# A six-stage decoder on one core: the column add of the switched attention moved by one batch, and other forms of the decay and the coupled attention

## The chip, the core and the metric

One core of a Trainium2 chip runs the whole program: TensorE multiplies, VectorE, ScalarE and GpSimd work elementwise, SyncE issues transfers, and semaphores order them. The metric is the device time of one execution in microseconds.

## The reference

Six layers follow each other, each with a residual and a layer normalisation. The text below is cut to the three attentions that the change touches.

```python
x = _layernorm(x + decay_attention(x))          # 16 batches, 112 tokens, 256 columns
x = _layernorm(x + cross_attention(x, ctx))
x = _layernorm(x + experts(x))
x = _layernorm(x + coupled_attention(x))
x = _layernorm(x + cross_attention(x, ctx))
x = _layernorm(x + switch_attention(x))

# decay attention, one head of 256 columns
qkv = x @ Wqkv + bqkv
attn = softmax(einsum('bqd,bkd->bqk', q, k) / sqrt(256) * mask)   # mask = gamma ** (i - j), 0 above the diagonal
out = einsum('bqk,bkd->bqd', attn, v) @ Wproj + bproj

# coupled attention, 16 heads of 16 columns
attn_scores = einsum('bhid,bhjd->bhij', Q, K) / scale
QJ = einsum('bhid,hde->bhie', tanh(Q), J_attn)
attn_scores = attn_scores + lambda_attn * einsum('bhie,bhje->bhij', QJ, tanh(K))
out = einsum('bhij,bhjd->bhid', softmax(attn_scores), V)          # then @ Wo.T + bo

# switched attention, 8 heads of 128 columns, 8 experts a head
gate_v, gate_o = two best of 8 sigmoid(x @ sel.T), normalised      # per token and head
v = einsum('bshep,bshe->bhsp', einsum('bsd,hedp->bshep', x, v_w), gate_v)
ctx = einsum('bhqk,bkhp->bqhp', softmax(q k^T * SCALE), v)
out = einsum('bshep,hepd->bsd', ctx[..., None, :] * gate_o[..., None], o_w)
```

## The kernel before

Each layer is a stage with its own tiles and semaphores, and a barrier stands between two stages. In a stage every engine has its own program, written out in the order in which it runs. `T` is 112 tokens, `B` 16 batches, `CB` 4 batches make a chunk of `CT` = 448 columns, and there are `NC` = 4 chunks.

**Decay attention** (`stage_decay_attention`, four chunks). TensorE's `step(c)` computes the scores of chunk `c` (L271), turns the normalised rows of chunk `c - 1` (`turn_out`, L263), projects queries, keys and values of chunk `c + 1` (`project`, L245 and L253), turns the probabilities (L280), multiplies them with the values (L287) and then with the output weights (L293). VectorE's `step(c)` makes the probabilities (L350 to L358), adds the output (L367), takes statistics and writes the rows `xn` (L380), all for chunk `c`. Chunks 1 and 2 run in a hardware loop. The decay mask is made by GpSimd at the start (L229).

**Coupled attention** (`stage_coupled_attention`, 16 batches in four groups of four heads). The scores of a group are two products into one bank: queries with masked keys (`km`, L1101), and the coupled queries `qj` with the masked tanh of the keys (`knm`, L1103). A mask keeps 16 of the 128 rows for each head, so that one product covers four heads. VectorE makes `km` (L1292, eight instructions a batch), ScalarE adds the biases to queries and keys (L1203, L1206) and makes `qn` (L1210) and `knm` (L1215, eight). `front` is the work on batch `b + 1`, `tail` that on batch `b - 1`; both are slipped in between the groups of batch `b`. GpSimd takes the inverse root of the variance (L1044) and copies rows (L1046).

**Switched attention** (`stage_switch`, 8 heads x 16 batches = 128 slots `g`). In a slot TensorE computes the values of one batch in two halves (`values(p, b, 0)` and `values(p, b, 1)`, six matmuls of 512 columns each), and between them twelve output matmuls of one unit (`outputs(u)`, a unit is two of the eight experts of one chunk). Large products are split in three (`split_product`, L104 to L106) from a high and a low part. Four units fill the two banks `OUTPUTS`. The units trail the values by two chunks: `gated_at(g)` is the unit whose gate product (`by_gates`, L2557) is made in slot `g`, `multiplied_at(g)` the unit that TensorE multiplies there. ScalarE rounds the gated product to `gh` (`high`, L2467), GpSimd takes the remainder `gl` (`low`, L2286). VectorE's `add_columns(n)` (L2565 for the first head, L2568 for the others) adds the banks to the columns `yt` once a chunk's four units are done, in the slot that `added_at` gives; TensorE's `outputs` waits for it (`y_read`) before the first unit of the next chunk. VectorE also scales and sums the values of a batch (L2523, then the halves in L2528 and L2532), and works through `choose`, the choice of the next head's gates, two steps a slot. `turned_at(g)` says when a chunk's columns are turned back to rows and normalised.

## Time and profile before

| what | us |
|---|---|
| median of 3 runs | 2683.79 |
| lowest, highest | 2677.88, 2686.36 |
| profiled execution | 2682.9 |
| its span | 2681.2 |
| decay attention in it, from 15.7 to 134 | 118.3 |
| coupled attention, from 970 to 1280 | 310 |
| switched attention, from 1690 to 2681 | 991 |

All rows below are of the profiled execution. Times are microseconds from the start of its span, and means are nanoseconds. A row of the timeline merges like instructions that follow each other; in brackets stands how long the engine was idle before it and what released it. A float32 matmul appears as two records. The granted clock of TensorE is 1.00 at 2.4 GHz and 0.50 at 1.2 GHz.

### The profile page before, as it was taken

The page shows a single profiled execution, that of the slowest core. Times are in us where ns is not written, and L with a number is a line of the kernel's source. Part 1 is how long each engine was busy: PE and PEld are TensorE (multiplying, and loading weights), DVE is VectorE, ACT ScalarE, POOL GpSimd, SP SyncE. Part 2 cuts the span into 40 slices and gives each one's busy share as a digit, 9 for nine tenths or more (in the row PEclk, how much of TensorE's full clock was granted, in tenths as well). Part 3 has the DMA queues.
Part 4 walks back from the last instruction along what each step waited for, and adds up shares of the span by engine and source line. Part 5 has one row for each costly group of instructions (what it writes and reads, how often), then busy time and mean ns, then how long its engine had stood idle before and what let it go on. Part 6 is the DMA issues. An engine that isn't in the chain of part 4 may idle for free. (4 is left out here: it accounts for less than half of the span.)

```text
span 2681.2 us, 48451 instructions
## 1 busy us (share of the span) xinstructions
PE 2334.2 (87%) x15579; PEld 1885.1 (70%) x15579; DVE 1741.8 (65%) x4378; ACT 1342.6 (50%) x3314; POOL 462.9 (17%) x382
## 2 busy tenths in 40 slices
PE   7689999869999868887799998889989998999995
PEld 5467777658999755554677776677777777777774
DVE  2356766657888556666467676767676676767555
ACT  2156666645666435554566666434343433434341
POOL 3010000011111320000100000022222323232223
PEclk9799999979999979999899999899999999999998
DMA  3056655224666210000565563232231322222222
GB/s 105 0 136 127 123 120 120 58 81 138 218 211 207 83 53 1 0 0 0 136 126 123 121 122 82 73 90 71 90 94 67 94 82 83 78 85 76 70 63 69
DMA packets 201755, 246.49 MB, mean 92 GB/s; under 512 B 58481, under 2 KB 176706, under 8 KB 201602
## 3 DMA queue, kind: packets, MB, share of 16 engines
q1 hardware_dynamic: 198050, 235.37, 33.6%
q0 software_dynamic: 3552, 9.18, 1.2%
q8 instruction: 84, 1.38, 0.2%
q14 instruction: 69, 0.57, 0.1%
HBM read 202.95 MB, written 41.55 MB: 91 GB/s over the span
## 5 line engine op out<-in xcount | busy, mean ns | idle before, releaser
L793 ACT ACTIVATE cross_pr<-cross_sc,cross_mn 112x375 f32<-112x375 f32 x512 | 310.5, 607 | 231.2 <-DVE cross_mn L883 230.2
L2286 POOL TENSOR_TENSOR switch_gl<-switch_gb,switch_gh 128x896 fp32r<-128x896 f32 x128 | 275.3, 2151 | 682.6 <-ACT switch_gh L2467 682.6
L883 DVE CUSTOM_DVE_ANT_0 cross_sc<-cross_ps,cross_masked 112x375 f32<-112x375 f32 x512 | 272.8, 543 | 177.0 <-PE cross_ps L681 156.1
L2523 DVE SCALAR_TENSOR_TENSOR switch_vt<-switch_ps,switch_chosen,switch_vt 112x128 f32<-112x128 f32 x512 | 144.3, 344 | 281.9 <-PE switch_ps L106 276.5
L104 PE MATMUL switch_ps<-switch_gh,switch_ow 128*128 128x448 f32 x512 | 202.9, 396 | 99.4 <-DVE switch_yt L2568 67.6
L689 PE MATMUL cross_ps<-all_ident,cross_pr 112*125 112x112 f32 x1536 | 255.2, 275 | 23.5 <-DVE cross_pt L890 21.7
L689 PEld LDWEIGHTS cross_ps<-all_ident,cross_pr 112*125 112x125 f32 x1536 | 232.7, 189 | 45.2 <-DVE cross_pt L890 27.7
L681 PE MATMUL cross_ps<-cross_k,cross_q 96*112 96x376 f32 x512 | 221.9, 434 | 14.1 <-DMA cross_k<-cross_k_dram 11.0
L104 PE MATMUL switch_ps<-switch_vw,switchgates_xh 128*112 128x512 f32 x512 | 211.6, 413 | 5.1 <-ACT switch_vt L2446 5.1
L106 PE MATMUL switch_ps<-switch_vw,switchgates_xl 128*112 128x512 f32 x512 | 203.5, 398 | 0.0
L105 PE MATMUL switch_ps<-switch_vw,switchgates_xh 128*112 128x512 f32 x512 | 203.5, 397 | 0.0
L106 PE MATMUL switch_ps<-switch_gh,switch_ow 128*128 128x448 f32 x512 | 200.9, 392 | 0.0
L105 PE MATMUL switch_ps<-switch_gl,switch_ow 128*128 128x448 f32 x512 | 200.6, 392 | 0.0
L104 PEld LDWEIGHTS switch_ps<-switch_gh,switch_ow 128*128 128x128 f32 x512 | 103.6, 202 | 126.8 <-issue 95.1
L2446 ACT ACTIVATE switch_vt<-switch_ps,switch_chosen 112x128 f32<-112x128 f32 x512 | 146.0, 367 | 93.3 <-PE switch_ps L106 93.3
L2467 ACT CAST switch_gh<-switch_gb 128x896 fp32r<-128x896 f32 x128 | 121.7, 950 | 47.3 <-DVE switch_gb L2557 38.0
L2557 DVE TENSOR_TENSOR switch_gb<-switch_gb,switch_ct 128x896 f32<-128x896 f32 x128 | 138.9, 1086 | 1.7 <-DMA switch_gb<-switch_gt_rows 1.6
L104 PE MATMUL experts_ps<-experts_xh,experts_w 128*128 128x256 f32 (+1 forms) x400 | 126.1, 315 | 8.2 <-ACT experts_h L1807 5.1
L890 DVE COPY cross_pt<-cross_ps 125x336 f32<-125x336 f32 x256 | 128.1, 500 | 1.6 <-PE cross_ps L689 1.5
L2021 DVE TENSOR_TENSOR experts_hl<-experts_h,experts_hh 128x256 fp32r<-128x256 f32 (+1 forms) x200 | 91.4, 457 | 55.3 <-ACT experts_h L1807 42.8
L625 POOL TENSOR_TENSOR cross_rstd<-cross_var,cross_half 112x1 f32<-112x1 f32 x32 | 17.3, 541 | 625.5 <-DVE cross_var L905 625.5
L104 PE MATMUL experts_ps<-experts_hh,experts_w 128*128 128x256 f32 (+1 forms) x400 | 122.7, 307 | 1.9 <-issue 1.9
(388 smaller groups left out, 5633.4 us busy)
## 6 DMA issues: line engine op xcount, KB each, us to landing
switch_gb<-switch_gt_rows SPq DMA_DIRECT2D x128, 448.0 KB, 3.6
experts_w_raw<-in_L_ffn_w_dram SPq DMA_DIRECT2D x42, 1024.0 KB, 5.7
cross_k<-cross_k_dram SPq DMA_DIRECT2D x96, 375.0 KB, 7.8
cross_k_dram<-cross_ks SPq DMA_DIRECT2D x32, 750.0 KB, 4.5
all_place<-in_ctx_dram SPq DMA_DIRECT2D x32, 375.0 KB
cross_q<-cross_q_dram SPq DMA_DIRECT2D x192, 56.0 KB, 4.4
all_place<-in_L_ffn_v_w_dram SPq DMA_DIRECT2D x16, 512.0 KB, 6.3
all_place<-in_L_ffn_o_w_dram SPq DMA_DIRECT2D x8, 1024.0 KB, 7.4
```

Source lines behind the costliest of these rows:

```text
L104: nc.tensor.matmul(out, w[0], x[0], start=first, stop=False)
L105: nc.tensor.matmul(out, w[0], x[1], start=False, stop=False)
L106: return nc.tensor.matmul(out, w[1], x[0], start=False, stop=last)
L681: nc.tensor.matmul(ps[0:T, SCORES + h % 2, 0:KEYS], q[parity][:, h // 2, h % 2, :], kk[parity][:, h // 2, :], start=True, stop=True).then_ ...
L689: last = nc.tensor.transpose(ps[0:KP, TURNED + h % 2, t * T:(t + 1) * T], pr[:, h % NB, t * KP:(t + 1) * KP], ident[0:T, 0:T])
L793: nc.scalar.activation(pr[:, h % NB, :], sc[:, h % NB, :], ACT.Exp, bias=mn[parity][:, h:h + 1], scale=-1.0, accum_out=rs[parity][:, h:h + ...
L883: nc.vector.tensor_tensor_reduce(out=sc[:, h % NB, :], in0=ps[0:T, SCORES + h % 2, 0:S2], in1=mask_of[:], scale=-0.25, scalar=3e38, op0=AL ...
L890: nc.vector.tensor_copy(pt[:, h % NB, :], ps[0:KP, TURNED + h % 2, 0:KT * T]).then_inc(pt_dve, 1)
L2286: pool.tensor_tensor(gl[u % 2][:], gb[u % RING][:], gh[u % 2][:].bitcast(F32), ALU.subtract)\
L2446: last = nc.scalar.activation(vt[b % 2][:, e, :], ps[0:T, VALUES, e * PW:(e + 1) * PW], ACT.Copy, scale=chosen[h % 2][:, b, e:e + 1])
L2523: last = nc.vector.scalar_tensor_tensor(out=part, in0=ps[0:T, VALUES + 1, e * PW:(e + 1) * PW], scalar=chosen[h % 2][:, b, EH + e:EH + e + ...
L2557: nc.vector.tensor_tensor(gb[u % RING][:], gb[u % RING][:], ct[n % 2][:].unsqueeze(1).broadcast_to([P, EU, CT]), ALU.mult).then_inc(gated, 1)
```

## The change

In the switched attention `added_at(g)` gives the slot in which TensorE multiplies the last unit, one slot earlier than before, and VectorE's `add_columns` moves behind the gate product and the steps of `choose` and ahead of `values`. `turned_at` gives one slot less for chunks 2 and 3.

In the coupled attention queries and keys share a tile `qk` with axes for half and kind. The rows of 64 partitions that four heads use hold queries and keys, and the other 64 partitions hold the coupled queries and the tanh of the keys for the same heads, so that one product of 128 rows gives the sum of both. VectorE adds the biases (two instructions of 64 partitions), ScalarE takes tanh of each half and writes the keys' to the other half, and GpSimd makes the masked keys of a batch in one instruction of 1792 columns (`masked_keys`), in front of the normalisation of batch `b - 1`.

In the decay attention the loop over chunks is written out. `project` is split in two, the turn of the rows of chunk `c - 1` stands behind both parts, and VectorE adds the output of chunk `c - 1` and takes its statistics in `step(c)`.

```diff
-    def project(c):
+    def project_queries_keys(c):
         pe.wait_ge(xs_ready, c + 1)
         for m in range(4):
+            if m == 2:
+                wait(pe, y_added, c - 1)
             for k in range(DC):
                 last = nc.tensor.matmul(ps[:, m, 0:CT], w[:, k, m * P:(m + 1) * P], xs[:, k, :],
                                         start=k == 0, stop=k == DC - 1)
             last.then_inc(qk_done, 1)
-        wait(pe, xt_ready, DC * c - DC)
+
+    def project_values(c):
...
         last.then_inc(s_done, 1)
-        if not first:
-            turn_out(c - 1)
         if not last_chunk:
-            project(c + 1)
+            project_queries_keys(c + 1)
+            project_values(c + 1)
+            pe.wait_ge(qk_ready, 4 * c + 8)
+            if not first:
+                turn_out(c - 1)
...
         pe.wait_ge(o_ready, DC * c + DC)
+        if not last_chunk:
+            wait(pe, xt_ready, DC * c)
...
+    def step(c, first, last_chunk):
+
+        ch = Chain(dve, chain, CB if first else CB + 9 + c * CHAIN - CHAIN)
+        dve.wait_ge(s_done, c + 1)
+        ch.link(nc.vector.tensor_tensor(sc[:], ps[0:T, 6, 0:CT].rearrange("p (a b) -> p a b", a=CB),
+                                        mask[:].unsqueeze(1).broadcast_to([T, CB, T]), ALU.mult))
+        ch.link(nc.vector.reduce_max(mx[:], sc[:], axis=AX.X))
+        nc.vector.tensor_tensor(sc[:], sc[:], mx[:].unsqueeze(2).broadcast_to([T, CB, T]),
+                                ALU.subtract).then_inc(shifted, 1)
+        if not first:
+            add_output(c - 1)
+        if last_chunk:
+            probabilities(c, ch)
+        if not first:
+            statistics(c - 1, ch)
+        if not last_chunk:
+            probabilities(c, ch)
+        if not first:
+            normalise(c - 1)
+            dve.wait_ge(xn_ready, c)
+        ch.link(nc.vector.tensor_tensor(y[:], x[:, ds(c * CB, CB), :],
+                                        y_bias[:].unsqueeze(1).broadcast_to([T, CB, D]), ALU.add))
+        if not last_chunk:
+            dve.wait_ge(o_done, DC * c + DC)
+            values(c + 1, ch)
+        else:
+            add_output(c)
+            statistics(c, ch)
+            normalise(c)
...
-k32 = s.sb("k32", [P, DC, T])
 qn = s.sb("qn", [P, DC, T])
-q = [s.sb(f"q{b}", [P, DC, T]) for b in range(2)]
-qj = [s.sb(f"qj{b}", [P, DC, T]) for b in range(2)]
-
-km = [s.sb(f"km{b}", [P, DC, HP, T]) for b in range(2)]
-knm = [s.sb(f"knm{b}", [P, DC, HP, T]) for b in range(2)]
+qk = [s.sb(f"qk{b}", [P, 2, DC, 2, T]) for b in range(2)]
+km = [s.sb(f"km{b}", [P, DC, 2, GH, T]) for b in range(2)]
...
+    def masked_keys(b, parity):
+        pool.wait_ge(ks_ready, b + 1)
+        whole = [P, 2 * DC, GH, T]
+        pool.tensor_tensor(km[parity][:].rearrange("p m i h t -> p (m i) h t"),
+                           qk[parity][:, 1].rearrange("p m i t -> p (m i) t").unsqueeze(2).broadcast_to(whole),
+                           head_mask[:, 0, :].unsqueeze(1).unsqueeze(3).broadcast_to(whole), ALU.mult).then_inc(k_ready, 1)
+
     def batch(b, parity, before, last):
+        if not last:
+            masked_keys(b + 1, 1 - parity)
...
-        c, h = g * GH // HP, g * GH % HP
-        bank = ps[0:T, SCORES + g % 2, 0:GH * T]
-        nc.tensor.matmul(bank, q[parity][:, c, :], km[parity][:, c, h:h + GH, :].rearrange("p a b -> p (a b)"),
-                         start=True, stop=False)
-        nc.tensor.matmul(bank, qj[parity][:, c, :], knm[parity][:, c, h:h + GH, :].rearrange("p a b -> p (a b)"),
-                         start=False, stop=True).then_inc(s_done, 1)
+        nc.tensor.matmul(ps[0:T, SCORES + g % 2, 0:GH * T], qk[parity][:, 0, g // 2, g % 2, :],
+                         km[parity][:, g // 2, g % 2].rearrange("p a b -> p (a b)"),
+                         start=True, stop=True).then_inc(s_done, 1)
...
             act.wait_ge(qk_ready, b + 1)
-            nc.scalar.activation(qn[:], q[parity][:], ACT.Tanh).then_inc(tanh_ready, 1)
-        elif u in (2, 3):
-
-            wait(act, s_done, (b - 1) * G)
-            for h in range((u - 2) * HP // 2, (u - 1) * HP // 2):
-                last = nc.scalar.activation(knm[parity][:, :, h, :], k32[:], ACT.Tanh, scale=head_mask[:, h:h + 1])
-            if u == 3:
-                last.then_inc(tanh_ready, 1)
+            for i in range(2):
+                rows_of = slice(i * HALF, (i + 1) * HALF)
+                last = nc.scalar.activation(qn[rows_of], qk[parity][rows_of, 0, :, i, :], ACT.Tanh)
+            last.then_inc(tanh_ready, 1)
+            for i in range(2):
+                last = nc.scalar.activation(qk[parity][(1 - i) * HALF:(2 - i) * HALF, 1, :, i, :],
+                                            qk[parity][i * HALF:(i + 1) * HALF, 1, :, i, :], ACT.Tanh)
+            last.then_inc(ks_ready, 1)
         else:
             act.wait_ge(j_done, b + 1)
-            nc.scalar.activation(qj[parity][:].rearrange("p a b -> p (a b)"), bank0[:, 0:DC * T], ACT.Identity,
-                                 scale=lam4[:]).then_inc(qj_ready, 1)
+            for i in range(2):
+                rows_of = slice((1 - i) * HALF, (2 - i) * HALF)
+                last = nc.scalar.activation(qk[parity][rows_of, 0, :, i, :],
+                                            bank0[rows_of, 0:DC * T].rearrange("p (a b) -> p a b", a=DC),
+                                            ACT.Identity, scale=lam4[rows_of])
+            last.then_inc(qj_ready, 1)
...
-            dve.wait_ge(qk_ready, b + 1)
-            for h in range(HP):
-                last = nc.vector.tensor_scalar(km[parity][:, :, h, :], k32[:], head_mask[:, h:h + 1], None, ALU.mult)
-            last.then_inc(k_ready, 1)
+            dve.wait_ge(qk_done, b + 1)
+            for i in range(2):
+                rows_of = slice(i * HALF, (i + 1) * HALF)
+                last = nc.vector.tensor_tensor(
+                    qk[parity][rows_of, :, :, i, :],
+                    ps[rows_of, FRONT, 0:2 * DC * T].rearrange("p (n m t) -> p n m t", n=2, m=DC),
+                    qk_bias[rows_of].unsqueeze(3).broadcast_to([HALF, 2, DC, T]), ALU.add)
+            last.then_inc(qk_ready, 1)
...
             shift(b, g, ch)
+            if not last and g == 1:
+                front(b + 1, 1 - parity, 1)
             if g >= 1:
                 total(b, parity, g - 1)
             elif before:
                 total(b - 1, 1 - parity, G - 1)
             if before and g == 1:
                 tail(b - 1, 1 - parity, 0, ch)
-            if not last and g in (1, 2):
-                front(b + 1, 1 - parity, g - 1)
+            if not last and g == 1:
+                front(b + 1, 1 - parity, 0)
...
-    u = gated_at(g - 2)
+    u = multiplied_at(g)
     return u // UNITS if u is not None and u % UNITS == UNITS - 1 else None
 
 def turned_at(g):
 
-    return {max(SLOTS + 1 + c, (LAST + c) * CB + 14): c for c in range(NC)}.get(g)
+    return {max(SLOTS + 1 + c, (LAST + c) * CB + 13): c for c in range(NC)}.get(g)
...
             by_gates(u)
-        n = added_at(g)
-        if n is not None:
-            add_columns(n)
         if p < HS:
             if b == QK_AT and p + 1 < HS:
                 weights_turned(p + 1)
...
                     next(steps, None)
             if b == 12:
                 assert next(steps, None) is None
+        n = added_at(g)
+        if n is not None:
+            add_columns(n)
+        if p < HS:
             values(p, b)
             if b in V_AT and p + 1 < HS:
                 raw, high_bits, low_bits = v_pieces((p + 1) % 2)[V_AT[b]]
```


How VectorE's order changes in the switched attention, at the slot of batch 4 in a head's cycle. `switch_gb` is the gated product, `switch_yt` the columns, `switch_vt` the scaled values, `switch_sel` and `switch_work` belong to `choose`. Before:

```order
L2557 TENSOR_TENSOR switch_gb<-switch_gb,switch_ct 128x896
L1373 TENSOR_REDUCE switch_second<-switch_gate 112x32
L1375 TENSOR_TENSOR switch_sel<-switch_gate,switch_second 112x256
L2523 SCALAR_TENSOR_TENSOR switch_vt<-switch_ps,switch_chosen,switch_vt 112x128 x4
L2528 TENSOR_TENSOR switch_v_half<-switch_vt 112x256
L2532 TENSOR_TENSOR switch_v<-switch_v_half 112x128
L2546 TENSOR_REDUCE switch_rs<-switch_pr 112x4
L2548 RECIPROCAL switch_ri<-switch_rs 112x4
L2550 TENSOR_TENSOR switch_pr<-switch_pr,switch_ri 112x448
L2557 TENSOR_TENSOR switch_gb<-switch_gb,switch_ct 128x896
L2568 TENSOR_TENSOR switch_yt<-switch_ps,switch_yt 128x2x448
```

Of the change:

```order
L2598 TENSOR_TENSOR switch_gb<-switch_gb,switch_ct 128x896
L1414 TENSOR_REDUCE switch_second<-switch_gate 112x32
L1416 TENSOR_TENSOR switch_sel<-switch_gate,switch_second 112x256
L2609 TENSOR_TENSOR switch_yt<-switch_ps,switch_yt 128x2x448
L2564 SCALAR_TENSOR_TENSOR switch_vt<-switch_ps,switch_chosen,switch_vt 112x128 x4
L2569 TENSOR_TENSOR switch_v_half<-switch_vt 112x256
L2573 TENSOR_TENSOR switch_v<-switch_v_half 112x128
```

The add of the columns moved up past seven instructions.

TensorE in the coupled attention, from the last projection of the next batch to the second group's scores and the work behind them. `coupled_pr` are probabilities, `coupled_osb` evacuated heads. Before:

```order
L1074 MATMUL coupled_ps<-coupled_xs,coupled_w 128x112 x4
L1101 MATMUL coupled_ps<-coupled_km,coupled_q 112x448
L1103 MATMUL coupled_ps<-coupled_knm,coupled_qj 112x448
L1110 MATMUL coupled_ps<-all_ident,coupled_pr 112x112 x4
L1082 MATMUL coupled_ps<-coupled_w,coupled_xs 112x256 x2
```

Of the change:

```order
L1119 MATMUL coupled_ps<-coupled_xs,coupled_w 128x112 x4
L1143 MATMUL coupled_ps<-coupled_km,coupled_qk 112x448
L1151 MATMUL coupled_ps<-all_ident,coupled_pr 112x112 x4
L1127 MATMUL coupled_ps<-coupled_w,coupled_xs 112x256 x2
L1168 MATMUL coupled_ps<-all_ident,coupled_osb 112x128 x4
```

The second product of a group's scores is gone.

TensorE in the decay attention, from the scores of chunk 1 on. Before, with rows of the loop:

```order
L271 MATMUL decay_ps<-decay_qk 112x112 x8
L263 MATMUL decay_ps<-all_ident,decay_xn 128x112 x8
L242 REGISTER_ALU
L245 MATMUL decay_ps<-decay_xs,first_w 128x448 x8
L88 ISA
L253 MATMUL decay_ps<-first_w,decay_xs 112x256 x8
L280 MATMUL decay_ps<-all_ident,decay_pr 112x112 x4
```

Of the change:

```order
L274 MATMUL decay_ps<-decay_qk 112x112 x8
L248 MATMUL decay_ps<-decay_xs,first_w 128x448 x8
L257 MATMUL decay_ps<-first_w,decay_xs 112x256 x8
L266 MATMUL decay_ps<-all_ident,decay_xn 128x112 x8
L285 MATMUL decay_ps<-all_ident,decay_pr 112x112 x4
```

The turn of the normalised rows moved from ahead of the projections to behind them.

## Rows read from the trace of the kernel before

**Rows 1.** Windows by stage: us, busy by engine (PE, PEld, DVE, ACT, POOL), clock, DMA.

```profile
15.70:134.00 118.30, 87.50 (x370) 62.41 (x371) 42.73 (x100) 26.26 (x44) 27.83 (x14) 0.84 0.11 34
...
970.00:1280.00 310.00, 255.54 (x1622) 163.00 (x1622) 188.12 (x465) 162.05 (x421) 22.58 (x46) 0.93 0.03 7
...
1690.00:2681.00 991.00, 870.65 (x4164) 729.47 (x4164) 659.70 (x1392) 376.27 (x848) 280.79 (x132) 0.95 0.26 80
```

**Rows 2.** Who waited for the tile of the columns, in us and times.

```profile
  PE switch_ps L104: 80.9, 30
```

**Rows 3.** Windows of three cycles of the switched attention, columns as in 1.

```profile
2068.99:2099.47 30.48, 27.16 (x128) 22.88 (x129) 21.07 (x45) 12.60 (x27) 8.59 (x5) 0.94 0.31 96
2099.47:2128.76 29.29, 27.14 (x128) 22.93 (x129) 20.03 (x43) 10.60 (x25) 8.50 (x4) 0.94 0.32 99
2128.76:2157.00 28.24, 26.11 (x134) 22.12 (x134) 17.92 (x38) 11.14 (x27) 8.49 (x4) 1.00 0.25 77
```

**Rows 4.** Timeline of TensorE around one wait: start, us, engine, line, operation.

```profile
1978.62 0.40 PE L106 MATMUL switch_ps<-switch_vw,switchgates_xl 128*112 128x512 f32 x1
1982.35 0.44 PE L104 MATMUL switch_ps<-switch_gh,switch_ow 128*128 128x448 f32 x1 [3.33 <-DVE switch_yt L2568]
...
1984.63 0.57 PE L104 MATMUL switch_ps<-switch_gh,switch_ow 128*128 128x448 f32 x1
1985.00 0.57 PE L105 MATMUL switch_ps<-switch_gl,switch_ow 128*128 128x448 f32 x1
```

**Rows 5.** Timeline of VectorE in the same stretch.

```profile
1975.29 1.13 DVE L2523 SCALAR_TENSOR_TENSOR switch_vt<-switch_ps,switch_chosen,switch_vt 112x128 f32<-112x128 f32 x4 [0.40 <-PE switch_ps L106]
1976.45 2.02 DVE L2528 TENSOR_TENSOR switch_v_half<-switch_vt 112x256 f32<-112x256 f32 x1
...
1981.12 1.08 DVE L2568 TENSOR_TENSOR switch_yt<-switch_ps,switch_yt 128x896 f32<-128x896 f32 x1
```

**Rows 6.** Timeline of GpSimd in the same stretch.

```profile
1976.06 2.13 POOL L2286 TENSOR_TENSOR switch_gl<-switch_gb,switch_gh 128x896 fp32r<-128x896 f32 x1 [5.53 <-ACT switch_gh L2467]
```

**Rows 7.** Window of one batch of the coupled attention, columns as in 1.

```profile
1103.91:1121.35 17.44, 14.96 (x101) 9.43 (x100) 11.73 (x29) 9.87 (x28) 0.94 (x2) 1.00 0.00 0
```

**Rows 8.** Timeline of TensorE at a group's scores in the coupled attention.

```profile
1121.35 0.92 PE L1101 MATMUL coupled_ps<-coupled_km,coupled_q 128*112 128x448 f32 x2
1122.10 0.91 PE L1103 MATMUL coupled_ps<-coupled_knm,coupled_qj 128*112 128x448 f32 x2
```

**Rows 9.** TensorE's waits in the coupled attention: us in total, times, longest.

```profile
PE coupled_ps L1144 <- DVE coupled_xn L1325: 14.9, 16, 2.5
PE coupled_ps L1138 <- ACT coupled_o L1244: 12.3, 15, 0.8
```

**Rows 10.** Groups by line in the coupled attention: busy, mean ns, idle before.

```profile
L1215 ACT ACTIVATE coupled_knm<-coupled_k,coupled_head_mask 128x224 f32<-128x224 f32 x128 | 50.7, 469 | 0.0
L1299 DVE TENSOR_REDUCE coupled_mx<-coupled_ps 112x4 f32<-112x448 f32 x64 | 39.7, 621 | 74.4 <-PE coupled_ps L1103 74.4
L1229 ACT ACTIVATE coupled_pr<-coupled_sc 112x448 f32<-112x448 f32 x64 | 36.7, 573 | 119.0 <-DVE coupled_sc L1301 118.6
L1292 DVE TENSOR_SCALAR coupled_km<-coupled_k,coupled_head_mask 128x224 f32<-128x224 f32 x128 | 32.7, 328 | 0.0
```

**Rows 11.** Timeline of TensorE in the decay attention.

```profile
30.05 6.19 PE L245 MATMUL decay_ps<-decay_xs,first_w 128*128 128x448 f32 x16
...
53.20 1.75 PE L263 MATMUL decay_ps<-all_ident,decay_xn 112*128 112x112 f32 x8 [4.40 <-DVE decay_xn L380]
54.75 8.16 PE L245 MATMUL decay_ps<-decay_xs,first_w 128*128 128x448 f32 x16
...
73.63 1.74 PE L271 MATMUL decay_ps<-decay_qk 128*112 128x112 f32 x16
...
100.61 1.73 PE L271 MATMUL decay_ps<-decay_qk 128*112 128x112 f32 x16
...
118.32 6.27 PE L293 MATMUL decay_ps<-first_wp,decay_o 128*112 128x256 f32 x16 [0.62 <-ACT decay_o L332]
```

110 lines of the change are left out of this document (50 added, 60 removed).

## The prediction

> **What bounds the kernel now.** I read four views in this order: busy time by stage, the waits of TensorE in the stages that the change touches, the windows of single cycles, and the timeline of all engines around one wait.
>
> The switched attention is 991 of the 2681 us, and TensorE is busy in 871 of them at a granted clock of 0.95; VectorE is busy in 660 [rows 1]. TensorE is the bound there, and what can be won is its idle time and its slow time. Nearly all the idle time is one wait: the first of the twelve output matmuls of a new chunk waits for the add of the last chunk's columns, 30 times, 80.9 us [rows 2], 2.7 us each. The timeline shows one: TensorE ends a batch's first value product at about 1979.0, idles 3.33 us, and goes on at 1982.35 [rows 4], just after the add began at 1981.12 and finished [rows 5]. But the products that the add reads ended before 1973.7: the add stood one batch late in VectorE's order. After such a wait the granted clock often falls: the output matmuls at 1984.63 and 1985.00 start 0.37 us apart [rows 4], where 0.20 is usual at 2.4 GHz; that is the 1.2 GHz level. The windows of three cycles of four batches have a clock of 0.94, 0.94 and 1.00 [rows 3].
>
> In the coupled attention an undisturbed batch takes 17.44 us, TensorE busy 14.96, VectorE 11.73, ScalarE 9.87 [rows 7]. TensorE's longest waits in total there are 14.9 us for the normalised row and 12.3 us for the evacuated heads [rows 9], both at the end of chains through VectorE, ScalarE and GpSimd.
>
> In the decay attention each chunk has one long wait of 4.40 us for the normalised rows, and the projection behind it takes 8.16 us, where the same sixteen records in the first chunk took 6.19 [rows 11].
>
> **Part 1, the add one batch sooner.** Nothing is added or removed: the add (1.08 us, 32 of them) moves from behind the next batch's gate product to ahead of this batch's value sums. Its input is done before TensorE's second value product, and after that come 2.4 us of queries and 1.4 us of the next first value product before the banks are wanted. In the cycle shown VectorE is free from 1974.9, starts the add at once and ends it at 1975.95, 3 us before TensorE asks at 1979.0. So the wait of 2.7 us goes, all of it, except that something else may be late next. Candidates are the split of the gated outputs (VectorE's gate product, ScalarE's rounding, GpSimd's remainder, 1.08 + 0.95 + 2.13 us in a row). GpSimd's row runs 1976.06 to 1978.19 [rows 6], before 1979.0: 0.7 us of slack for the first unit. The value sums start 0.65 us later than at 1975.29 [rows 5], but the halving sum behind them was already held until GpSimd was through (2.02 us instead of 0.42 [rows 5, 6]), so the delay is swallowed, and the next gate product still ends at 1981.15. From there 1.0 for ScalarE and 2.2 for GpSimd give 84.5; TensorE, no longer waiting, asks for it at 78.9 + 2.45 (outputs) + 1.4 + 0.4 (transposes) + 1.4 = 84.5. The unit after that comes out at 90.65 against 90.7. So the chain is level with TensorE in the tight cycles, and I charge 0.5 us of new wait to half of the 30 cycles: +8. In the cycles where VectorE computes a long reciprocal first, the add ends 1.3 us after its old neighbour began and TensorE still comes 2.5 us later.
>
> Gain in waits: 80.9, of which 1.3 lies in the drain at the end: 79.6. Gain in clock: (1 - 0.94) x 30.48 + (1 - 0.94) x 29.29 + 0 over three cycles is 3.6 us, 1.2 a cycle [rows 3]; for the stage 991 x 0.05 = 50 us [rows 1] bounds it from above, with slow stretches at the start and in the drain that stay. I take 1.1 x 29 = 32. The turn of chunks 2 and 3 one slot earlier takes one statistics block of VectorE out of the way of the last gate product: I take -3. Part 1: -79.6 - 32 + 8 - 3 = -107 (from -90 if the clock returns for only half, to -118 with no new wait and all of the clock).
>
> A rule of the Trainium skill bears on it ("SBUF — State Buffer", Who interferes with whom): a VectorE instruction with two SBUF inputs and a GpSimd instruction that reads SBUF exclude each other for the whole instruction, the first one wins. The 2.02 us row agrees. By that rule the moved add, which reads one operand from PSUM, blocks nobody, and the sum stays without a term for it.
>
> **Part 2, coupled attention.** Scores take one product instead of two: a group's product costs 0.75 us (1121.35 to 1122.10 [rows 8]), so 4 x 0.75 = 3.0 us of TensorE go per batch: 14.96 becomes 11.96. ScalarE loses the eight masked tanh rows and four bias rows [rows 10] and is no bound. VectorE loses the key masks (eight rows of 0.26 us start to start, 2.04), and gets two additions from PSUM, unseen before; the nearest row is the 448-column reduction at 0.62 [rows 10], so +1.2, and 11.73 becomes 10.9. GpSimd gets the masks of the keys, 1792 columns a batch; its nearest row is 896 columns in 2.13 us [rows 6], so 4.2 us; from below VectorE's 1.4 ns a column (0.62 us for 448 [rows 10], so 2.5 us), from above twice its own row for the two repeated operands (8.5 us). I take 4.2, since the row is of the same engine and kind.
>
> Now the order: from the end of the second group's scores VectorE does shift 1.25, the new additions 1.2, sum 0.55, reciprocal and heads 0.65, values 0.4, and only then the shift of the third group, ready at 5.45 (before: 4.7). ScalarE's exponent (0.57) ends at 6.1, then 0.45 + 0.7 (scaled products) + 0.3 to the heads, 7.6; output product to 8.55. The keys: additions at 2.65, tanh twice for queries and twice for keys to 4.05, GpSimd to 8.3: ready 0.25 us before the next batch's scores want them. Then VectorE's statistics to 10.4, GpSimd's root to 10.95, the normalised row at 11.4; the shift of the new first group, queued behind it, 12.6; exponent 13.1, evacuation 13.6, values, projection, and the second group's scores end at 15.65. So 17.44 becomes 15.65: of the 3.0 us 1.2 come back as waits (1.8 instead of 0.8 us for the normalised row). GpSimd's queue: the root stands behind the masks, which end two microseconds earlier, so no charge. The additional idle time may lower the clock: two of the three cycles in [rows 3] lost 1.8 us of it behind waits of 2 to 3 us; at one in two, 0.9 per batch. Per batch -0.9, 15 batches: -14; the start gets GpSimd's 4.2 us in line in place of eight tanh rows: +2. Part 2: -12. Ends: -25 (clock stays up), +33 with the masks at 8.5 us (3.8 us per batch on the way, 19.5 a batch).
>
> **Part 3, decay attention.** The normalised rows of a chunk are turned behind the next projection instead of before it. VectorE needs 8.1 us from the scores to the rows (three rows of 0.65, add 1.25, statistics 2.0, sums 1.5, rows 1.4; all its work is 42.7 / 4 = 10.7 us a chunk [rows 1]), TensorE has 9.5 us of projection in between, so the wait of 4.40 goes, and with it the slow projection (8.16 - 6.19 = 2.0). New: the third projection waits for the add, 0.5. A chunk of 26.98 (73.63 to 100.61 [rows 11]) becomes 21; two such: -12. The last chunk has nothing to put between: scores 1.74, wait 5.0 for add and probabilities, then 0.55 + 0.7 + 2.0 + 0.6 + 3.7 = 14.3, 15 with some slow clock, against 24.0 from 100.61 to 118.32 + 6.27 [rows 11]: -9. The start is set by the mask, unchanged. Part 3: -21 (-14 to -24).
>
> **Sum.** -107 - 12 - 21 = -140. The profiled execution took 2682.9 us (span 2681.2), the median of the runs is 2683.8, so the one stands for the other: 2682.9 - 140 = 2543.
>
> **Rivals.**
> (a) The split of the gated outputs becomes the bound of the switched attention. For it: level in the tight cycles, and VectorE rows that hold GpSimd. Against: GpSimd is busy 281 of 991 us [rows 1]. At 0.6 us more in three of four batches of each of 30 cycles: +54, 2597.
> (b) The key masks on GpSimd cost twice the row. Coupled +33 instead of -12: 2588.
> (c) The clock stays low for other reasons: -32 becomes 0 and the decay keeps 4: 2579.
> (d) The change doesn't do what it says: the add is held by work ahead of it on VectorE, so that only half of the waits go. -40 - 16 in place of -112 in Part 1: 2599.
> (e) Slower: one mechanism, the key masks on GpSimd. Scores of the next batch wait 4.05 us + the masks' time m, and 7.1 us follow, so a batch takes 11.15 + m once m exceeds 4.5. The other parts give -128; that is used up at 17.4 + 8.5 = 26 us a batch, m = 15 us, seven times as long as the row of 2.13 us says per column. At m = 20 it is 31.2 a batch, +206: 2761. Nothing in [rows 6] points there.
>
> **How the numbers follow.** Forecast 0.75, (a) 0.07, (b) 0.07, (c) 0.04, (d) 0.03, (e) 0.02; 0.02 for something unseen with no change in sum or a loss. The forecast's own bounds add to 2516 (-118, -25, -24) and 2572 (-90, 0, -21 or so). The range takes in (b) and (c): 2515 to 2590, and leaves out (a), (d), (e) and the outer ends. Under 0.3% (8 us) a measurement of this kernel tells nothing from no change; faster 0.97, same 0.01, slower 0.02.
>
> **What would show it.** Right: no wait of the output matmuls for the column add except in the drain; cycle windows of 25.5 to 26.2 us at clock 1.00 where 28.2 to 30.5 stood; the switched stage near 884 us; coupled batches of 15.6 to 16.5 us with a single 4.2 us row on GpSimd; decay chunks of 21 us with no wait before the turn. Wrong: waits of the output matmuls for GpSimd's remainder above 1 us each; masks above 6 us; coupled batches with a clock below 0.9; the column add starting after TensorE's next first value product.

## The result and the profile after

The changed kernel takes 2537.7 us (median of 4 runs, 2536.0 to 2539.0) against 2681.9 for the kernel before: a ratio of 0.946 (95% interval 0.944 to 0.948), 144 us less. Forecast were 2543, range 2515 to 2590. The profiled execution has a span of 2535.6 us.

The table by stage answers to [rows 1]: the decay, the coupled and the switched attention of the changed kernel. Each line is a stretch, its length, the busy time of each engine, the granted clock of TensorE and the DMA's share.

```profile
core 0: us, PE busy (x) PEld busy (x) DVE busy (x) ACT busy (x) POOL busy (x), PEclk, DMA share, GB/s
15.60:113.50 97.90, 80.91 (x368) 58.15 (x369) 42.26 (x100) 24.65 (x43) 29.52 (x11) 0.90 0.14 41
956.00:1238.50 282.50, 226.42 (x1469) 150.98 (x1470) 173.90 (x363) 122.95 (x287) 64.84 (x46) 0.86 0.03 8
1662.00:2535.00 873.00, 836.39 (x4164) 707.66 (x4164) 630.64 (x1392) 374.61 (x846) 276.32 (x132) 0.98 0.29 91
...
```

Between the same landmarks before and after, the switched stage shrank from 988.8 to 873.4 us (-115.4; its first split product to the end of the span), the coupled one from 292.8 to 282.5 (-10.3; a batch's first projection to the last output product), the decay attention from 115.6 to 96.5 (-19.1; first projection to last turn of rows). The stages between moved by 1 us or less. In the switched stage TensorE has the same 4164 matmuls; its busy time falls from 870.7 to 836.4, which is the clock's share, and its idle time in the windows from 120 to 37.

In the middle of that stage nothing is left to gain from waits. One stretch of 700 us:

```profile
1740.00:2440.00 700.00, 700.00 (x3542) 595.83 (x3542) 514.24 (x1121) 320.11 (x723) 232.38 (x110) 1.00 0.30 92
```

TensorE shows as busy for all of it, at full clock. Its waits in the whole stage up to 2520 (who waited for whom: total, times, longest) answer to [rows 2]:

```profile
PE switch_ps L104 <- POOL switch_gl L2327: 17.2, 7, 5.6
PE switch_ps L104 <- ACT switch_vt L2487: 4.9, 2, 2.5
PE switch_ps L104 <- DVE switch_qkw L2554: 2.5, 1, 2.5
PE switch_ps L104 <- DVE switch_yt L2609: 1.3, 1, 1.3
```

The 30 waits for the column add (80.9 us) are down to one, in the drain. The waits for GpSimd's remainder lie outside the 700 us, at the start and in the drain, where the longest, 5.6, stands. One add and the work around it in the timeline of the engines other than TensorE (start, duration), and the next add; they answer to [rows 5, 6]:

```profile
2040.81 1.09 DVE L2609 TENSOR_TENSOR switch_yt<-switch_ps,switch_yt 128x896 f32<-128x896 f32 x1 [0.50 <-PE switch_ps L106]
...
2041.86 2.13 POOL L2327 TENSOR_TENSOR switch_gl<-switch_gb,switch_gh 128x896 fp32r<-128x896 f32 x1 [5.28 <-ACT switch_gh L2508]
...
2043.35 0.91 DVE L2569 TENSOR_TENSOR switch_v_half<-switch_vt 112x256 f32<-112x256 f32 x1
...
2045.91 1.08 DVE L2598 TENSOR_TENSOR switch_gb<-switch_gb,switch_ct 128x896 f32<-128x896 f32 x1
...
2048.14 2.13 POOL L2327 TENSOR_TENSOR switch_gl<-switch_gb,switch_gh 128x896 fp32r<-128x896 f32 x1 [4.15 <-ACT switch_gh L2508]
...
2068.24 1.09 DVE L2609 TENSOR_TENSOR switch_yt<-switch_ps,switch_yt 128x896 f32<-128x896 f32 x1
```

The first output products behind them, on TensorE, with no wait:

```profile
2045.83 0.36 PE L104 MATMUL switch_ps<-switch_gh,switch_ow 128*128 128x448 f32 x1
...
2051.97 0.37 PE L104 MATMUL switch_ps<-switch_gh,switch_ow 128*128 128x448 f32 x1
```

The cycle between the adds took 27.43 us, the ones before and behind it 24.40 and 25.39, all at clock 1.00, where 28.2 to 30.5 stood in [rows 3]. Four in a row, from the add of 2220.93 to that of 2323.22, take 102.3, 25.6 each.

The cycle shown is the roomiest of four kinds that follow each other up to 2373. From the adds of 2040.81, 2068.24, 2093.63 and 2118.68, the add ends 3.9, 2.4, 2.4 and 2.9 us before TensorE takes up the banks, and the second remainder behind it ends 1.7, 0.6, 0.1 and 0.1 us before its product. The prediction worked with the cycle whose add stood at 1981.12 before; its counterpart now is this one, of the last kind:

```profile
1914.13 1.09 DVE L2609 TENSOR_TENSOR switch_yt<-switch_ps,switch_yt 128x896 f32<-128x896 f32 x1
...
1915.27 2.13 POOL L2327 TENSOR_TENSOR switch_gl<-switch_gb,switch_gh 128x896 fp32r<-128x896 f32 x1 [5.53 <-ACT switch_gh L2508]
...
1916.29 1.39 DVE L2569 TENSOR_TENSOR switch_v_half<-switch_vt 112x256 f32<-112x256 f32 x1
...
1918.05 0.36 PE L104 MATMUL switch_ps<-switch_gh,switch_ow 128*128 128x448 f32 x1
...
1919.32 1.08 DVE L2598 TENSOR_TENSOR switch_gb<-switch_gb,switch_ct 128x896 f32<-128x896 f32 x1
...
1921.46 2.13 POOL L2327 TENSOR_TENSOR switch_gl<-switch_gb,switch_gh 128x896 fp32r<-128x896 f32 x1 [4.06 <-ACT switch_gh L2508]
...
1923.74 0.44 PE L104 MATMUL switch_ps<-switch_gh,switch_ow 128*128 128x448 f32 x1
```

The second remainder is through at 1923.59 and its product starts at 1923.74, 0.34 us behind the start of the product before it, where 0.23 is the step of that row of products. So in this kind of cycle the split is level with TensorE, and costs it about 0.1 us.

Coupled attention, TensorE around the turn of the normalised row (L1185), and the next turn. It answers to [rows 8] and [rows 9]:

```profile
1079.16 0.92 PE L1143 MATMUL coupled_ps<-coupled_km,coupled_qk 128*112 128x448 f32 x2
1079.91 0.55 PE L1151 MATMUL coupled_ps<-all_ident,coupled_pr 112*112 112x112 f32 x4
1081.97 0.41 PE L1185 MATMUL coupled_ps<-all_ident,coupled_xn 112*128 112x112 f32 x2 [1.51 <-DVE coupled_xn L1364]
1082.31 0.40 PE L1160 MATMUL coupled_ps<-coupled_pt,coupled_v 112*32 112x112 f32 x8
...
1098.75 0.41 PE L1185 MATMUL coupled_ps<-all_ident,coupled_xn 112*128 112x112 f32 x2 [1.50 <-DVE coupled_xn L1364]
```

The same batches as windows from turn to turn:

```profile
1064.19:1081.97 17.78, 14.81 (x93) 9.92 (x93) 10.97 (x24) 7.61 (x18) 4.11 (x3) 0.81 0.00 0
1081.97:1098.75 16.78, 13.65 (x92) 9.25 (x92) 10.90 (x24) 7.61 (x18) 4.11 (x3) 0.90 0.00 0
1098.75:1116.53 17.78, 14.99 (x92) 10.11 (x92) 10.91 (x24) 7.61 (x18) 4.11 (x3) 0.81 0.00 0
1116.53:1132.46 15.93, 12.17 (x92) 7.99 (x93) 10.91 (x24) 7.61 (x18) 4.11 (x3) 1.00 0.00 0
```

At clock 1.00 a batch takes 15.93, but the mean of four is 17.07: the clock costs 1.14 a batch. Before, twelve batches took 212.6 us, 17.7 each: ten of 17.4 at clock 1.00 and two of 19.10 at 0.91. So a batch gained 0.65 us, of the 3.0 us of product that went.

Decay attention, TensorE at the scores of the third chunk and from those of the last one on, against [rows 11]:

```profile
66.21 1.74 PE L274 MATMUL decay_ps<-decay_qk 128*112 128x112 f32 x16
...
85.98 1.74 PE L274 MATMUL decay_ps<-decay_qk 128*112 128x112 f32 x16
92.48 0.60 PE L285 MATMUL decay_ps<-all_ident,decay_pr 112*112 112x112 f32 x4 [4.76 <-DVE decay_pr L386]
93.69 3.75 PE L290 MATMUL decay_ps<-decay_pt,decay_v 112*128 112x112 f32 x16 [0.62 <-ACT decay_pt L338]
...
110.30 1.75 PE L266 MATMUL decay_ps<-all_ident,decay_xn 112*128 112x112 f32 x8 [5.18 <-DVE decay_xn L378]
```

A middle chunk takes 19.8 us where 26.98 stood. The value products of the last chunk take 3.75 where each other chunk's take 2.04: behind the wait of 4.76 the granted clock of the stretch from 93.69 to 104.35 is 0.55.

### The profile page after: what moved, and what is told of

Read it like the earlier page. It is cut to its first block and busy times, and to the rows that moved or that the text cites. A ratio compares the mean times of both kernels' runs of the same rounds, so it can differ in the third digit from the quotient of the medians.

```text
span 2535.6 us, 47865 instructions
## 1 busy us (share of the span) xinstructions
PE 2269.8 (90%) x15451; PEld 1853.6 (73%) x15451; DVE 1701.2 (67%) x4282; ACT 1306.0 (52%) x3186; POOL 510.4 (20%) x399
## 5 line engine op out<-in xcount | busy, mean ns | idle before, releaser
L723 PE MATMUL cross_ps<-all_ident,cross_pr 112*125 112x112 f32 x1536 | 256.6, 276 | 23.6 <-DVE cross_pt L924 22.3
L104 PE MATMUL switch_ps<-switch_gh,switch_ow 128*128 128x448 f32 x512 | 192.4, 376 | 18.5 <-POOL switch_gl L2327 17.2
L106 PE MATMUL switch_ps<-switch_gh,switch_ow 128*128 128x448 f32 x512 | 190.4, 372 | 0.0
L105 PE MATMUL switch_ps<-switch_gl,switch_ow 128*128 128x448 f32 x512 | 190.4, 372 | 0.0
L2062 DVE TENSOR_TENSOR experts_hl<-experts_h,experts_hh 128x256 fp32r<-128x256 f32 (+1 forms) x200 | 91.4, 457 | 54.2 <-ACT experts_h L1848 43.3
L715 PEld LDWEIGHTS cross_ps<-cross_k,cross_q 96*112 96x112 f32 x512 | 91.2, 179 | 47.5 <-issue 28.0
L104 PEld LDWEIGHTS switch_ps<-switch_gh,switch_ow 128*128 128x128 f32 x512 | 98.2, 192 | 37.9 <-POOL switch_gl L2327 19.9
```

The lines of the kernel that those rows point to most:

```text
L104: nc.tensor.matmul(out, w[0], x[0], start=first, stop=False)
L105: nc.tensor.matmul(out, w[0], x[1], start=False, stop=False)
L106: return nc.tensor.matmul(out, w[1], x[0], start=False, stop=last)
L715: nc.tensor.matmul(ps[0:T, SCORES + h % 2, 0:KEYS], q[parity][:, h // 2, h % 2, :], kk[parity][:, h // 2, :], start=True, stop=True).then_ ...
L723: last = nc.tensor.transpose(ps[0:KP, TURNED + h % 2, t * T:(t + 1) * T], pr[:, h % NB, t * KP:(t + 1) * KP], ident[0:T, 0:T])
```

## The experiments

Theory: the three parts work each in its own stage and add; in the switched attention both the waits and the clock came back, and the chain that splits the gated outputs (VectorE's gate product, ScalarE's rounding, GpSimd's remainder) has room (which held in one kind of cycle of four); in the coupled attention a chain through several engines, not TensorE, sets the batch. Rivals stand in the expectations. Where a run is compared with the changed kernel, the changed kernel ran beside the second group of runs: 2537.4 us, 0.9455 (0.944 to 0.947). The kernel before, which ran beside every group, took 2682.2 to 2682.9 there and in the later groups, and 2675.2 in the first.

**Each part alone.** Edit of the first: the switched stage's hunks of the diff; of the others: the coupled and the decay stage's hunks.

> The kernel before with the switched attention's two edits alone (the column add one batch sooner, the turn of chunks 2 and 3 one slot earlier); the coupled and the decay attention as before. Theory (the parts add, each stage keeps its own gain): the switched stage took 988.8 us before and 873.4 with the whole change, so 2682 - 115 = 2567 us, with the granted clock 1.00 in the cycles and no wait of the output matmuls for the column add outside the drain. Rival (part of the stage's gain comes from what stands ahead of it, in that the other two parts change the state in which the stage starts): the prediction's own -107 or less, 2575 us or more. Rival (the gain is the waits alone, the clock recovers for other reasons): -80, 2602 us.

> The kernel before with the coupled attention's new form alone (one score product a group, the key masks on GpSimd). Theory: the stage took 292.8 us before and 282.5 with the whole change, so 2682 - 10 = 2672 us; batches of 15.9 to 17.8 us where 17.44 stood, one 3.2 us row of masks on GpSimd a batch. Rival (the prediction's sizes, batches of 15.65 us and 0.9 us of slow clock, none of it lost elsewhere): -12 to -14, 2669 us. Rival (the gain of the stage is paid back in the cross attention behind it): 2682 us.

> The kernel before with the decay attention's new order alone (the turn of the normalised rows behind the next projection). Theory: the start of the next stage came 20.2 us sooner with the whole change, 1.1 of them from the load; so 2682 - 19 = 2663 us, two middle chunks of 19.8 us where 26.98 stood and a last chunk of 18.4 us to the end of its output product. Rival (the sooner end of the stage meets weights of the cross attention that are not yet loaded, or a slower clock there): -10 or less, 2672 us.

Measured: 0.9562 (0.954 to 0.958), 0.9965 (0.9955 to 0.9975) and 0.9926 (0.991 to 0.994) of the kernel before: -117, -9.4 and -19.8 us by these ratios. They add to -146, against -144 and -146 for the whole in its two comparisons. The rivals that let one stage pay for another fall: the parts are independent. (The interval of the second, -7 to -12, just touches its rival of -12.) The first alone has the switched stage of the whole change: 873.5 us, TensorE busy 836.3, clock 0.98. The rival "waits alone" (-80) falls too: 34 us came from the clock.

**The changed kernel again, and the turn in the drain.** The first is the same file. The edit of the second:

```diff
-            return {max(SLOTS + 1 + c, (LAST + c) * CB + 13): c for c in range(NC)}.get(g)
+            return {max(SLOTS + 1 + c, (LAST + c) * CB + 14): c for c in range(NC)}.get(g)
```

> The changed kernel again, on the chip of the runs beside it, as their measure. Theory: 0.946 of the kernel before, as in its first comparison.

> The changed kernel with the turn of chunks 2 and 3 in the drain back at its old slot. The prediction gave that edit 3 us: 3 us slower than the changed kernel. Rival (the edit is worth nothing, or costs, because VectorE's statistics now stand ahead of a gate product that TensorE waits for): 0 or 3 us faster.

Measured: 0.9455 both, medians 0.2 us apart. The edit is worth nothing that shows, where the prediction gave it 3 us. In the drain, from 2480 on, TensorE waits 13.3 us for remainders with the old slot and 11.7 with the new one.

**How much room the add and the split have.** I took the room from the cycle shown first: the add of 2040.81 ends at 2041.90 and TensorE wants the banks at 2045.83; the next remainders end at 2043.99 and 2050.27 and are wanted at 2045.83 and 2051.97. The expectations rest on this cycle alone, the roomiest kind. I delayed VectorE by rows that nobody reads.

```diff
                 if n is not None:
+                    for i in range(2 if n < LAST else 0):      # 4 in the other
+                        nc.vector.tensor_tensor(spare[:], x[:, 0:4, 0:224], x[:, 4:8, 0:224], ALU.add).then_inc(spare_done, 1)
+                        dve.wait_ge(spare_done, n * 2 + i + 1)
                     add_columns(n)
```

> The changed kernel, with two rows of VectorE (896 columns, two operands in SBUF, about 1.1 us each) put in front of each of the 28 column adds ahead of the drain, into a tile that nothing reads; it delays the add and all that VectorE does behind it by 2.3 us. In the changed kernel the add ends 3.9 us before TensorE wants the banks, and the split remainders end 1.6 to 1.8 us before TensorE wants them. Theory (both slacks hold, VectorE's own idle time takes up the rest of the delay before the next gate product): 0 to +5 us against the changed kernel. Rival (the prediction's picture, the split chain level with TensorE): each cycle is 1.5 to 2.3 us longer, +42 to +64 us and the clock with it.

> As with two such rows, but four, 4.5 us. Theory: now the add is 0.65 us late and the next gate product's remainder, after VectorE's idle time, another 1.35, so 2.0 us a cycle in 28 cycles, +56 us, with 1.1 us of slow clock a cycle +87 us against the changed kernel. Rival (only the add's own slack counts): 0.65 us a cycle, +18 us.

Measured: 0.9635 (0.962 to 0.965), +49 us, and 0.9986 (0.997 to 1.000), +142 us against the changed kernel. The theory of both runs missed; the first came out in the range of its rival (+42 to +64), which has the split level with TensorE. From 1700 to 2480 TensorE waited 17.6 us for the add and 24.0 for remainders with two rows, 80.1 and 5.5 with four. In the whole stage its busy time rose from 836.4 to 847.7 and 887.1: with four rows the slow clock is back, 51 of the 142 us. One cause of the misses was in the rows themselves (line, count, duration min/median/max; then one pair beside a remainder of GpSimd):

```profile
L2666 DVE TENSOR_TENSOR switch_spare<-all_x x56: 1083/1092/2906, 1733.4 to 2473.3; 112x896 f32<-112x896 f32 x56
```

```profile
2009.78 4.02 DVE L2666 TENSOR_TENSOR switch_spare<-all_x 112x896 f32<-112x896 f32 x2
2010.51 2.35 POOL L2329 TENSOR_TENSOR switch_gl<-switch_gb,switch_gh 128x896 fp32r<-128x896 f32 x1 [5.55 <-ACT switch_gh L2510]
```

A row of 1.09 us, two operands in SBUF, was held until GpSimd's remainder was through: the pair took 4.02 in place of 2.2. So the delay was up to 4 us, not 2.3. The other cause was the room: where 2.4 us stood before the banks are wanted and the pair took 4.0, TensorE waited 1.3 to 1.6 for the add; in the cycles of the kind of 2040.81 it did not wait at all. The last run takes the held rows out by reading PSUM:

```diff
                 dve.wait_ge(unit_done, (n + 1) * UNITS)
                 banks, cols = ps[:, OUTPUTS:OUTPUTS + DC, 0:CT], yt[:, :, c * CT:(c + 1) * CT]
+                for i in range(2 if n < LAST else 0):
+                    nc.vector.tensor_copy(spare[:], banks).then_inc(spare_done, 1)
+                    dve.wait_ge(spare_done, 2 * n + i + 1)
```

> The changed kernel, with two rows of VectorE that copy the output banks (PSUM) to a tile that nothing reads, in front of each of the 28 column adds ahead of the drain, behind the add's own wait: 2.3 us, as with the two rows from SBUF, but with no operand in SBUF. Theory (the two rows from SBUF cost 49 us because some of them were held to 2.9 us by GpSimd's remainder, which used up both slacks; a row that reads PSUM is not held, and 2.3 us fit in the add's slack of 3.9 and, after VectorE's idle time, in the remainder's slack of 1.7): 0 to +10 us against the changed kernel, all these rows at 1.09 us. Rival (it is the length of VectorE's work alone, 2.3 us is more than the chain of the split has to spare): +35 to +49 us.

Measured: 0.9576 (0.956 to 0.959), +31 us. Between both expectations. The rows, and TensorE's waits from 1700 to 2480:

```profile
L2608 DVE COPY switch_spare<-switch_ps x56: 1083/1091/1092, 1734.2 to 2454.6; 128x896 f32<-128x896 f32 x56
```

```profile
PE switch_ps L104 <- POOL switch_gl L2329: 26.9, 21, 1.5
...
PE switch_ps L104 <- DVE switch_yt L2611: 0.7, 1, 0.7
```

None of the 56 rows was held, and the add was late once: 2.2 us fit into its 2.4. The remainder was late 21 times, by 1.28 in the mean. Between the adds of 1763 and 2377 it was late once in each cycle of the three kinds that had 0.6 us of room or less, by 1.1 to 1.5, and never in a cycle of the fourth kind, with 1.7. VectorE's idle time took up less than 1 us of the delay. The two pairs of rows differ by 18 us (16 by the ratios), which is about what the held operands cost; the pairs also stand on different sides of the add's wait, and ran beside different groups.

**Where the coupled attention's gain went.** First the wait alone is moved away: TensorE turns the normalised row later.

```diff
                     if g == 0:
-                        if before == 2:
-                            tail(b - 2, 3)
                         if before:
                             values(b - 1, 1 - parity, G - 2)
                         if not last:
                             front(b + 1, 1 - parity, 0, (0,))
+                        if before == 2:
+                            tail(b - 2, 3)
```

> The changed kernel, but in the coupled attention TensorE turns the normalised row behind the value product of the third group and the first half of the next projection, instead of ahead of them. Theory (the 1.5 us wait for the normalised row is only the place where a longer chain shows: the next value product waits for a copy of ScalarE that stands behind the exponent of the new first group, and that exponent follows the normalised row on VectorE, so that the idle time moves to that product): a batch stays at 17.1 us, 0 to -3 us. Rival (the wait is a loss by itself): 1.5 us and the slow clock behind it, 2.6 a batch over 14 batches, -36 us against the changed kernel.

Measured: 0.9452 (0.944 to 0.947), -1.3 us. TensorE's waits in the stage:

```profile
PE coupled_ps L1160 <- ACT coupled_pt L1269: 28.6, 15, 2.0
...
PE coupled_ps L1185 <- DVE coupled_xn L1364: 5.7, 3, 2.5
```

The 25.4 us of wait for the normalised row in the changed kernel became 5.7, and the wait for ScalarE's copy of the turned group rose from 6.9 to 28.6. The rows of the changed kernel behind one normalised row show why:

```profile
1081.50 0.41 DVE L1364 TENSOR_SCALAR coupled_xn<-coupled_y,coupled_mv,coupled_rstd 112x256 f32<-112x256 f32 x1 [0.66 <-POOL coupled_rstd L1078]
...
1082.57 0.62 DVE L1340 TENSOR_TENSOR coupled_sc<-coupled_ps,coupled_mx 112x448 f32<-112x448 f32 x1
...
1083.36 0.58 ACT L1264 ACTIVATE coupled_pr<-coupled_sc 112x448 f32<-112x448 f32 x1 [4.03 <-DVE coupled_sc L1340]
1083.84 0.51 ACT L1269 COPY coupled_pt<-coupled_ps 112x448 f32<-112x448 f32 x1
...
1084.41 0.60 PE L1160 MATMUL coupled_ps<-coupled_pt,coupled_v 112*32 112x112 f32 x8
```

The copy's input, the turned group, was there since 1080.5 (its turn by L1151 starts at 1079.91); ScalarE sat idle for 4.03 us in front of the exponent, which waited for VectorE. Then the copy is put ahead of the exponent, with the turn moved as well:

```diff
-                    exponent(b, g)
                     if g >= 1:
+                        exponent(b, g)
                         evacuate(b, g - 1)
-                    elif before:
-                        evacuate(b - 1, G - 1)
+                    else:
+                        if before:
+                            evacuate(b - 1, G - 1)
+                        exponent(b, g)
```

> As the kernel with the turn later, and ScalarE copies the turned fourth group ahead of the exponent of the new first group instead of behind it. Theory (the chain is cut, the 1.5 us of idle time go and so does most of the slow clock that follows it, 1.1 us in a mean batch): -20 to -36 us against the changed kernel, batches near 15 us at a clock over 0.95. Rival (another chain of VectorE, ScalarE and TensorE is next within half a us): -7 us or less.

Measured: 2492.8 us, 0.9285 (0.927 to 0.930), -44.6 against the changed kernel, more than the upper estimate, and -43.3 against the run with the turn alone, from which it differs by this one edit. (The copy moved without the turn was not run.) The copy now follows its input directly, and two batches as windows from turn to turn show no slow clock:

```profile
1104.87 0.53 ACT L1269 COPY coupled_pt<-coupled_ps 112x448 f32<-112x448 f32 x1 [1.24 <-PE coupled_ps L1151]
```

```profile
1092.42:1106.26 13.84, 12.10 (x92) 7.99 (x92) 10.92 (x24) 7.62 (x18) 4.11 (x3) 1.00 0.00 0
1106.26:1120.11 13.85, 12.11 (x93) 8.00 (x93) 10.92 (x24) 7.61 (x18) 4.12 (x3) 1.00 0.00 0
```

TensorE has the same 12.1 us of work, its idle time fell from 3.8 to 1.7, and the twelve full batches all have clock 1.00: 17.07 to 13.84, 3.2 us in 14 batches, 45. The chain was: normalised row, the shift of the new group behind it on VectorE, exponent, copy, value product on TensorE, and around to the next normalised row. This version is faster than both kernels.

The same two moves in the kernel before:

> The kernel before (two products per score group, key masks on VectorE and ScalarE), with TensorE's turn of the normalised row and ScalarE's copy moved in the coupled attention as in the kernel with both moved. Theory (the chain through normalised row, exponent and copy was there before as well, 0.76 + 0.62 us of TensorE's idle time in an undisturbed batch): 16.1 us a batch where 17.44 stood and 17.7 in the mean, 14 batches, -23 us against the kernel before, 2659 us; the new form of the coupled attention would then be worth 2.2 us a batch in place of 0.65. Rival (before the change TensorE was the bound and the chain hardly counted): -5 us or less.

Measured: 0.9888 (0.987 to 0.991), 2654.7 us, -27.5, where 23 were expected. Batches take 15.77 us (turns at 1082.62, 1098.39, 1114.16), TensorE busy in 14.68 of them. So the chain was there before, and TensorE was close behind it. With the chain uncut the new form of the coupled attention is worth 9.4 us. With it cut it is 15.77 - 13.84 = 1.9 us a batch; from the comparisons, if their gains add, -9.4 - 44.6 + 27.5 = -26.5 us.

**The key masks on GpSimd, three times over.** Two more such rows stand ahead of the real one:

```diff
                 pool.wait_ge(ks_ready, b + 1)
+                for n in range(2):
+                    pool.tensor_tensor(km_extra[n][:], ...)      # the operands of the row below
                 pool.tensor_tensor(km[parity][:].rearrange("p m i h t -> p (m i) h t"),
```

> The changed kernel, with two more of the same key-mask rows on GpSimd ahead of the real one in every batch, into tiles that nothing reads: 9.5 us of masks a batch in place of 3.17. Theory (the prediction's rival (e) as a rule, a batch is 11.15 us + the masks' time once that exceeds 4.5): 20.7 us a batch where 17.1 stood, +54 us against the changed kernel, and TensorE's scores wait for GpSimd in every batch. Rival (the masks lie on the chain already at 3.17 us, each of their 6.3 additional us shows): +95 us. Rival (the wait for the masks takes the place of the wait for the normalised row, 1.5 us of it, and the clock no longer falls further): +30 us.

Measured: 0.9735 (0.971 to 0.976), +75 us. Two of its batches from score to score, and TensorE's waits:

```profile
1098.33:1118.96 20.63, 13.67 (x92) 8.65 (x93) 13.94 (x23) 7.61 (x18) 10.50 (x6) 0.83 0.00 0
1118.96:1139.60 20.64, 13.65 (x92) 8.65 (x93) 13.94 (x23) 7.61 (x18) 10.52 (x6) 0.83 0.00 0
```

```profile
PE coupled_ps L1149 <- POOL coupled_km L1091: 91.4, 16, 9.7
```

The masks took 9.6 us, and 11.15 + 9.6 = 20.7: rival (e)'s rule holds in ten of the thirteen full batches (20.6 to 20.7), and the rival that every additional microsecond shows (+95) falls. The other three took 23.42 at a granted clock of 0.72, which the rule does not have. The thirteen batches took 54 us more than in the changed kernel, near the expected sum, of which 8 are those three. Another 19 us stand ahead of the first turn of a normalised row (1015.29 against 995.90): TensorE's waits for the masks there are 22.3 us in place of 4.5, and my expectation left them out.

## Why the prediction was right, point by point

**Part 1** (-107 forecast, -115 in the stage, -117 by itself). The waits: 79.6 forecast; TensorE's idle time between the two windows fell by 84 us, of which 2 stand ahead of the stage's first product. The clock: 32 forecast, 34 measured as TensorE's busy time. The working of the tight cycle was right almost to the row. In its counterpart (1914.13 to 1923.74 above) the add ends 2.8 us before TensorE's products, 3 worked out; the first remainder 0.65 before them, 0.7 worked out; the second 0.15 before its own, level in the working; the halving sum is held for part of the moved add's delay, as it said (1.39 where 2.02 stood), and the next gate product ends 2.35 us behind the start of those products, as worked out. What failed is the price put on it: the charge of 0.5 us in half of the cycles, +8, had no row behind it. Level costs nothing, or here 0.1, and no wait shows between 1740 and 2440. The waits and the clock together without the charge, -112, are within 5 us of what was measured. By the Trainium skill ("SBUF — State Buffer", Who interferes with whom) a VectorE instruction with two SBUF inputs contends with a GpSimd instruction that reads SBUF, and one with at most one SBUF input, outside the two-port modes, does not. The trace agrees: 56 rows from PSUM at 1.08 to 1.09 us each, 56 rows with both operands in SBUF at up to 2.91. How near rival (a) was, the delayed kernels show: 2.2 us more on VectorE make the remainder late 21 times. The -3 for the turn in the drain was wrong: 0. Rivals (a), (c) and (d) did not come about.

**Part 2** (-12 forecast, -10.3 in the stage, -9.4 by itself). The sum is close, for partly wrong reasons. The batch at full clock: 15.65 forecast, 15.93 measured; the wait for the normalised row 1.8 and 1.5; TensorE's work 11.96 and 12.17. The masks: 4.2 forecast, 3.17 measured, below the row I took it from by column; that left rival (b) no ground. The clock: 0.9 forecast, 1.14 measured. One of the prediction's own signs of being wrong came true: two batches of four have a clock of 0.81, below its 0.9, and only one of four lies in its 15.6 to 16.5 us. Mis-sized was the base: 17.44 is an undisturbed batch, the mean of before is 17.7, so a loss to the clock was left out before, and too little of it was put in after. That the two largely cancel is luck. And the step that is only half right is what the wait is. The prediction wrote "1.2 come back as waits" and followed the chain up to the second group's scores, but spoke of the wait for the normalised row as the price. The runs show that moving that wait alone gives 1 us, and moving ScalarE's copy as well another 43.

**Part 3** (-21 forecast, -19.1 in the stage, -19.8 by itself). The middle chunks gained 7.2 us each, not 6 (19.8, not 21: the third projection waits 0.2, not 0.5, and none of it is at slow clock). The last chunk, 85.98 to the end of its output product at 104.35, took 18.4, not 15: the wait was as forecast (4.8, 5.0), but the products behind it ran slow (3.75 for 2.04, 6.28 for 3.71), 4.3 us for which "some slow clock" had 0.7. The same products were slow before, 6.27 in [rows 11]; the working put 3.7 for them. The errors of the middle and the last chunks partly cancel.

**Rival (e)** had a rule that did not come into play: masks of 3.17 us are below the 4.5 from which it decides, and tripled masks followed it to 0.1 us in ten batches of thirteen. Its "seven times as long as the row says per column" is a slip: 15 us is seven times the row of 2.13 itself, and 3.5 times its price per column, so the loss was nearer than the text has it.

## What to carry to other kernels

The engine that an idle row names is where a chain surfaces, and need not be what sets it. Before crediting or moving a wait, follow what the waiting step releases and see whether it comes around to itself through another engine's queue. Here, with the wait already moved for 1 us, one copy put ahead of one exponent on ScalarE gave 43 us; left where it was, it also ate most of the work that the new form had removed from TensorE. An instruction that stands late in its queue with inputs long ready can be cheap to win: one moved add and its clock were worth 117 of the 144 us. Move it only as far as the next chain has room, and measure that room in every kind of cycle: the first one shown here had 1.7 us, its neighbours 0.1 to 0.6. A delay row that is to measure it should leave the other engines alone, as the rows from PSUM did.

## What the runs showed of the hardware

- What a wait does to TensorE's clock differs by stage. In the coupled attention of the changed kernel, waits of 1.5 us beside shorter ones came with clocks of 0.81 to 1.00 in successive batches of equal work; with the longest wait of a batch at 0.65 it stayed at 1.00. In the switched attention of the run with PSUM rows, 21 waits of 1.3 us left it at 1.00; with four SBUF rows, waits of 1.7 to 4.2 us for the add came with 0.95 (1740 to 2600). The stretch of the run with PSUM rows:

```profile
1740.00:2460.00 720.00, 694.65 (x3492) 585.88 (x3491) 573.77 (x1163) 315.72 (x715) 228.37 (x108) 1.00 0.27 89
```

- GpSimd's masks, 1792 columns with two repeated operands, took 3.17 us, 1.8 ns a column; its remainder, 896 columns, 2.13 us, 2.4 ns a column. When three mask rows stood in a row, the median rose to 3.35.
- VectorE's column add took 1.08 us before and 1.09 after: the move did not change its own time.
